# Recurrent layer of a four-layer kernel: chunks of 8 tokens in place of 16

## The reference

```python
def step(carry, x):
    vec, St = carry
    ...
    pred = jnp.einsum('bhij,bhi->bhj', St, kt)
    delta = vt - pred
    S_new = at[..., None, None] * St + bt[..., None, None] * (kt[..., :, None] * delta[..., None, :])
    read = jnp.einsum('bhij,bhi->bhj', S_new, qt)
    return ((vec_new, S_new), (vec_new, read))
_, (vec_states, reads) = jax.lax.scan(step, (vec0, S0), xs)
```

## Time and profile before

| | us |
|---|---|
| median of three runs | 1208.66 |
| profiled execution, its own time | 1207.07 |
| span of that execution on the core | 1205.2 |
| DVE busy | 867.5 (72%) |
| PE busy | 674.5 (56%) |
| ACT busy | 506.5 (42%) |
| POOL busy | 403.4 (33%) |

### The profile page before, as it was taken

How to read it: one execution, slowest core, us unless ns; L and a number is a source line. 1 busy time by engine, 2 the same in 40 slices (tenths; PEclk the granted TensorE clock), 3 DMA queues, 4 the chain that set the end, 5 groups by cost and what they waited for, 6 DMA issues and landing times.

```text
span 1205.2 us, 11485 instructions
## 1 busy us (share of the span) xinstructions
PE 674.5 (56%) x4014; PEld 333.1 (28%) x4014; DVE 867.5 (72%) x1306; ACT 506.5 (42%) x752; POOL 403.4 (33%) x334
## 2 busy tenths in 40 slices
PE   4990000040004004479899799963264799978997
PEld 2450000040004003222222556631243122225655
DVE  6899999999999995856657733269959557667212
ACT  3423000122220001579999322243034899973321
POOL 1250847600006602226765000006802566650000
PEclk9985555555555556779999799987565899997999
DMA  2250006172000020223310000000003242100001
GB/s 92 70 140 1 1 0 140 35 168 63 13 14 14 0 35 0 84 75 116 97 33 22 1 1 1 1 0 1 0 0 115 63 142 54 54 1 1 1 1 35
DMA packets 30258, 50.71 MB, mean 42 GB/s; under 512 B 4472, under 2 KB 14328, under 8 KB 29176
## 3 DMA queue, kind: packets, MB, share of 16 engines
q1 hardware_dynamic: 29432, 49.32, 15.2%
q10 hardware_dynamic: 768, 0.66, 0.3%
HBM read 20.98 MB, written 16.92 MB: 31 GB/s over the span
## 4 chain that ended last, share of the span: by engine, by line
DVE 47%; PE 23%; ACT 16%; issue 10%; POOL 1%; DMA 1%; ACTq 1%; POOLq 0%; SPq 0%; DVEq 0%
ACT PX L1445 10%; PE PS L1330 6%; PE PS L1308 5%; PE PS L1350 4%; PE PS L1289 3%; DVE D L813 2%; DVE S L817 2%; DVE P L814 2%; DVE PS L871 2%; DVE PRD L870 2%; DVE mag L1031 2%; DVE PA L772 2%; ACT P L688 2%; DVE RO L837 2%; DVE RP L832 2%
## 5 line engine op out<-in xcount | busy, mean ns | idle before, releaser
L1445 ACT ACTIVATE PX<-PS 128x1024 f32<-128x1024 f32 (+1 forms) x320 | 268.1, 1016 | 12.1 <-PE PS L1271 12.1
L1224 POOL TENSOR_TENSOR PX<-PX,maskf 128x256 f32<-128x256 f32 (+1 forms) x192 | 173.4, 931 | 125.0 <-ACT PX L1445 124.5
L1289 PE MATMUL PS<-PX,VA 128*32 128x512 f32 (+3 forms) x1536 | 166.2, 503 | 22.3 <-POOL PX L1224 14.5
L1617 DVE SCALAR_TENSOR_TENSOR X<-PS,wts,X 128x96 f32<-128x96 f32 x128 | 38.4, 315 | 118.2 <-PE PS L1350 103.9
L1271 PE MATMUL PS<-QS,KS 64*128 64x512 bf16 (+3 forms) x768 | 107.8, 339 | 16.7 <-issue 11.4
L1554 DVE RECIPROCAL DEN<-DEN 128x512 f32<-128x512 f32 x32 | 107.3, 3353 | 1.1
L580 PE MATMUL PS<-ones,HT 64*128 64x1 f32 x64 | 13.0, 348 | 152.0 <-ACT HT L672 152.0
L947 POOL TENSOR_TENSOR PRQ<-PA,LQK 128x2048 f32<-128x2048 f32 (+15 forms) x16 | 39.9, 2520 | 151.8 <-DMA WS<-S 138.6
L1552 DVE LOAD_MASK_SELECT DEN<-PS x32 | 0.4, 14 | 107.2 <-PE PS L1289 93.5
L591 PE MATMUL PS<-awout,V 64*128 64x128 f32 x64 | 13.3, 422 | 110.5 <-DVE vss L820 110.5
L1308 PE MATMUL PS<-HT,fw 128*128 128x512 f32 x144 | 71.2, 638 | 3.9 <-DVE HG L1584 2.6
(11 more groups left out here) (264 smaller groups left out, 1649.5 us busy)
## 6 DMA issues: line engine op xcount, KB each, us to landing
QS<-qs_d SPq DMA_DIRECT2D x32, 196.0 KB
qs_d<-QP SPq DMA_DIRECT2D x24, 256.0 KB, 3.9
ks_d<-QP SPq DMA_DIRECT2D x24, 256.0 KB, 4.0
KS<-ks_d SPq DMA_DIRECT2D x32, 192.0 KB
K<-LQK SPq DMA_DIRECT2D x16, 256.0 KB
W<-WS SPq DMA_DIRECT2D x16, 256.0 KB, 4.1
qkv_d<-CY SPq DMA_DIRECT2D x3, 1024.0 KB, 3.9
LQK<-qkv_d SPq DMA_DIRECT2D x8, 256.0 KB, 4.9
```

The source lines that it names most:

```text
L1224: pool.tensor_tensor(block, block, bcast(maskf[:], 1, 2 * halves), ALU.mult).then_inc(probs_masked, 1)
L1289: last = pe.matmul(PS[32 * h:32 * h + 32, SCORES_BANKS + qc, c0:CH], VA[b][:, kt, h, :], px[:, i % 2, at:at + CH - c0], start=(kt == 0), s ...
L1445: act.activation(tile(PX[u % PDEPTH][:]), tile(PS[:, k:k + 2, :]), ACT.Exp).then_inc(probs_ready, 1)
```

## The change

The chunk is 8 tokens instead of 16. `NC` follows (32 in place of 16), and so do all loops over `C` and `NC`. `READ_TURNS` gets one sum behind each of the eight columns. A tile `BELOW` is added that nothing uses: it moves the address of `GAM` up, because tiles of this stage lie over tiles of an earlier one.

```diff
-SEG, C = 4, 16
+SEG, C = 4, 8
...
                         LA = sb("LA", [P, NC, C, C], at=s2)
+                        BELOW = sb("BELOW", [P, 2 * S + 2 * S + P], at=s2)
...
-        READ_TURNS = [(0,), (1, 2), (3, 4), (5, 6), (7, 8, 9), (10, 11), (12, 13), (14, 15)]
+        READ_TURNS = [(j,) for j in range(C)]
```

## The result

The changed kernel takes 1186.68 us (median of 4 runs, 1185.2 to 1189.81); the kernel before, on the same chip, 1208.45 (4 runs, 1207.18 to 1212.03). The ratio is 0.9829, with a 95% interval from 0.9809 to 0.9849. A second measurement on another chip gave 0.9831 (0.9806 to 0.9855, experiment e9). The forecast was 1187, ratio 0.982.

What follows compares the result with a forecast made beforehand. DVE's list of instructions was taken to bound layer A's stages. Terms of -72.3 and +50.8 us gave -21.5, taking 1207.07 to 1185.6; 1.6 more for the median gave 1187 us, range 1180 to 1195.

Steps and rivals of the forecast that it cites:

- The law: DVE's time in layer A: 1.043 ns per element plus a fixed part, 0.19 us per chained instruction whatever its size.
- Four terms: Layer A: Gram -29.0 us, solve of the keys -20.2, solve of three value columns -9.4, scan +49.7.
- The rival of the slower scan: Scan: a step of half the elements still takes nearly 1.88 us, kernel up to 1258 us; chance 0.05.
- The forecast's count for this rule: Whole kernel, counting instructions alone: +256 in the scan, about -70 elsewhere at 0.19 us, some +35 us, 1244.
- The rival of the late transfers: Scan start: waits for `W2`, `U2` or POOL's solve, up to 5 or 6 us, total 1192; chance 0.06.
- 1.0 in the sum: Scan start: DVE's second instruction waits for ACT's copy of `U2`, about +1.0 us, between 0 and 1.5.
- The rival of dear rows: Scan: writing `P2` in shorter rows costs more per element, 11.6 us, total 1199; chance 0.03.
- The scaling of `LA`: Scaling behind Gram: 7 instructions over 896 elements instead of 15 over 1920, -1.7 us.
- that of `PA`: Scaling before the scan: 8 instructions over 1152 elements instead of 16 over 2176, another -1.7 us.
- From scan to reads: End of the scan: the last states are transfers of twice the size, +0.1 us.
- The reads: Reads: 8 sums over POOL's products instead of 16, and no 1.10 us wait for POOL, -10.3 us.
- stay hidden under the tree: Tree: POOL's decays, 8 instructions instead of 16, run beside it and were given no term in the sum.

Runs made afterwards that it cites:

- e9: The changed kernel itself, unaltered, measured again on another chip: 1187.04 us, ratio 0.9831 to the kernel before.
- e2: The kernel before, with chunks of 16 in all other stages, but each scan step cut into two of 8 tokens: 1259.6 us.
- e1: The changed kernel with chunks of 4 tokens instead of 8, and states kept partly in a second idle tile: 1270.33 us.
- e3: The changed kernel with POOL's decays started only when DVE has finished the tree: 1188.87 us.
- e5: The kernel before, chunks of 16, with POOL's decays started only when DVE has finished the tree: 1205.65 us.
- e8: The changed kernel with DVE's Gram products reading the keys from SBUF instead of the copy in PSUM: 1190.46 us.

## Why the prediction was right

**The law held.** Four terms were worked out from 1.043 ns per element and 0.17 to 0.19 us per chained instruction (0.08 for Gram's sums that are not waited for). Gram came out 0.2 us longer than forecast, the two solves 0.05 longer and 0.1 shorter. The scan, the one stage that grows and the largest single doubt, took 170.87 - 0.72 = 170.15 us of steps against 169.9, and e2 gave it alone. The doubt was that its instructions had been seen only at twice the size; e1 shows that the same two prices hold at a quarter.

**The rival of the slower scan.** It needed a step above 1.50 us; the step is 1.33. The Trainium skill, Advanced Engine Details and Errata, section The Read-Write Bubble, advises large tiles. The trace agrees that each instruction has a fixed price, but the verdict depends on the elements that smaller tiles save beside it. The forecast's count for this rule was a little off: outside the scan 80 instructions went, not about 70 (1482 - 1306 = 256 - 80), which makes it 33 us instead of 35. Going from 16 to 8 the triangles lose more than the scan gains in instructions. Going from 8 to 4 the law turns against the smaller tile: Gram, both solves and the reads save only 33 us more (28.40 to 14.38, 25.84 to 11.00 and 47.56 to 43.02), while the scan, counted from its first sum on, loses 100 (169.85 to 269.96).

**The rival of the late transfers.** The wait was 0.72 us, against 1.0 in the sum, within the 0 to 1.5. The chain was the one named: ACT's copy, four issues of 2.41 us in all, then a landing. The page counts a landing from the start of an issue, and so counted the last one took the 2.0 us of the earlier trace rows. The forecast's 30.7 to 31.3 us from the solve's start left open from where to count; at its upper end the last issue is in the sum twice. The transfer landed at 185.2, 30.7 us from the solve's start, so the lower end was right and the 1.0 taken from the middle was 0.3 too much. `W2` was no hindrance at this size, though `K2` had left SP's queue only 0.7 us before it (173.33 and 174.06), while e1 shows it as the main wait one size further.

**The rival of dear rows.** Line 815, which writes rows of 8 at a pitch of 9, takes 0.29 us, as long as line 811 with rows of the same kind and as long as the solve's instruction of 128 elements in the earlier trace rows. There is nothing dear in them.

**POOL.** Its solve was forecast to end 22 us into the stage, ahead of DVE's 26.0. It ended 22.0 us in, at 176.53, and DVE's at 180.35. Its first product in Gram made DVE wait 0.65 us; forecast 0.6.

**What the forecast had wrong, all of it small.** The scaling of `LA` gained 1.6 us, not 1.7, and that of `PA` 1.6. From scan to reads 0.17 us were added, not 0.1. The reads gained 10.10 us, not 10.3. These terms together give -20.99 us in place of -21.5. Two things were not in it. The tree became 1.03 us shorter: the sentence that POOL's decays "stay hidden under the tree" took hidden work for free work, and e3 and e5 show that moving it away is worth 2.47 us before and 1.44 after. And the last stretch was 754.16 us, 1.27 longer than the 752.89 that the span of before leaves from the same place on. This is no effect that I can lay to the change: from the statistics of the next layer to the end, the eight kernels e1 to e8, whose code there is the same, had 739.9 to 745.3 us, with 742.0 before and 744.2 after. The two nearly cancel, so part of the agreement of the total (20.9 us measured, 21.5 forecast) is luck of about a microsecond. The stages are the better test than the sum.

## What to carry to other kernels

Fit a stage's time to elements and instructions before choosing a block size. Quadratic work inside a block and a serial chain across blocks then price each other, and for 16, 8 and 4 the two numbers name the best size here. When a stage gets shorter, look up what its length had covered: first a transfer of 0.72 us, one size further one of 12.80 us. And a stage hidden on another engine is free only if the two engines do not hold each other up: here moving it behind the tree, where it runs four times as fast, was worth more than a microsecond of the engine that sets the end.

## What the runs showed of the hardware

DVE and POOL can block each other for whole instructions. Beside DVE's products of 3072 elements, whose inputs both lie in SBUF, POOL instructions of 16 to 48 elements (before) and 32 to 96 (after) took 2.8 to 3.4 us, and the same ones 0.25 to 0.41 when DVE was in one-input work (e3, e5). DVE is held up too: in e8 its product of 1536 elements took 3.23 us instead of 1.74. With one DVE input in PSUM (Gram, after) no such lengthening is seen: DVE's first product took 2.02 us with POOL beside it, and POOL's second 3.97, against 3.96 in e8, where it ran beside one-input sums and held DVE's next product up. DVE's sums with one input lost none in e8. So where an operand lies decided 5.52 us of Gram, though no single instruction's own price depends on it: the first product took 2.03 us from SBUF and 2.02 from PSUM.

The Trainium skill, SBUF — State Buffer, section "SBUF: two separate sides", says that DVE and GpSimd (here POOL) share a pair of ports which one instruction holds exclusively until it ends, and that a DVE operation with two SBUF inputs takes part in it against a GpSimd operation that reads SBUF. The traces agree: 6.27 us for POOL's product is its own 4.51 and nearly the whole of what remained of DVE's.
